# Cross-attention and a mixture of experts on one core: each group's attention starts four slots earlier in the order of work, the second group's in the head

## What is computed

```python
q = layernorm(x) @ Wq.T                      # [*, 128]
k = v = ctx @ Wq.T
x = x + softmax(causal(q @ k.T / sqrt(128))) @ v          # within each sequence of 64
n = layernorm(x)
gates = softmax(n @ gate_W)                  # 8 experts
cw = the two largest gates, divided by their sum, 0 elsewhere
out = n + sum_e cw[:, e] * (relu(n @ W1[e] + b1[e]) @ W2[e] + b2[e])   # hidden width 256
x = x + out
```

## Time and profile before

| | us |
|---|---|
| median of 3 runs | 143.75 (143.26 to 143.96) |
| profiled execution, its own time | 143.2 |
| span of that execution | 141.4 |
| PE busy | 125.1 (88%) |
| DVE busy | 104.9 (74%) |
| ACT busy | 96.2 (68%) |
| POOL busy | 47.3 (33%) |

### The profile page before, as it was taken

How to read it: one execution, slowest core, us unless ns; L and a number is a source line. 1 busy time by engine, 2 the same in 40 slices (tenths; PEclk the granted TensorE clock), 3 DMA queues, 4 the chain that set the end, 5 groups by cost and what they waited for, 6 DMA issues and landing times. The chain is left out here.

```text
span 141.4 us, 3259 instructions
## 1 busy us (share of the span) xinstructions
PE 125.1 (88%) x1165; PEld 92.9 (66%) x1165; DVE 104.9 (74%) x413; ACT 96.2 (68%) x191; POOL 47.3 (33%) x53
## 2 busy tenths in 40 slices
PE   6987079789999699999998799999996999699992
PEld 2774055658786457887875468697864677467781
DVE  1529999998559799476586995885497994978573
ACT  3346354976959486796959476769685848689940
POOL 6380342703033750330127532130336603333500
PEclk9999956999999999999999999999999999999999
DMA  3999900000000000200000001000000002000002
GB/s 107 293 270 270 270 4 5 0 0 2 0 5 0 0 7 0 74 0 5 0 0 0 0 5 53 28 0 0 0 5 2 2 5 74 0 2 5 0 0 74
DMA packets 9872, 5.54 MB, mean 39 GB/s; under 512 B 472, under 2 KB 9856, under 8 KB 9856
## 3 DMA queue, kind: packets, MB, share of 16 engines
q1 hardware_dynamic: 9712, 5.27, 12.9%
q10 hardware_dynamic: 144, 0.07, 0.2%
HBM read 4.28 MB, written 1.05 MB: 38 GB/s over the span
## 5 line engine op out<-in xcount | busy, mean ns | idle before, releaser
L623 POOL TENSOR_TENSOR h_lo<-h,h_hi 128x512 f16<-128x512 f32 x24 | 27.9, 1162 | 67.7 <-ACT h L517 67.7
L517 ACT ACTIVATE h<-psH,b1T 128x512 f32<-128x512 f32 x64 | 43.5, 686 | 3.1 <-PE psH L347 1.8
L790 DVE SCALAR_TENSOR_TENSOR acc<-psY,weight_y,acc 128x128 f32<-128x128 f32 x125 | 35.1, 342 | 5.8 <-PE psY L368 5.3
L516 ACT ACTIVATE h_hi<-psH,b1T 128x512 f16<-128x512 f32 x48 | 33.0, 687 | 9.1 <-PE psH L347 9.0
L774 DVE TENSOR_TENSOR h_lo<-h,h_hi 128x512 f16<-128x512 f32 x24 | 17.3, 721 | 15.2 <-ACT h L517 15.2
L347 PE MATMUL psH<-x_lo,w_hi 128*128 128x512 f16 x62 | 23.8, 384 | 0.4
L343 PE MATMUL psH<-x_hi,w_hi 128*128 128x512 f16 x62 | 23.8, 384 | 0.0
L344 PE MATMUL psH<-x_hi,w_lo 128*128 128x512 f16 x62 | 23.8, 383 | 0.0
L368 PE MATMUL psY<-w_hi,h_hi 128*128 128x128 f16 x192 | 22.7, 219 | 0.0
L368 PE MATMUL psY<-w_lo,h_hi 128*128 128x128 f16 x192 | 22.7, 219 | 0.0
L368 PEld LDWEIGHTS psY<-w_hi,h_hi 128*128 128x128 f16 x192 | 15.4, 98 | 3.3
(11 more groups left out here) (169 smaller groups left out, 184.3 us busy)
## 6 DMA issues: line engine op xcount, KB each, us to landing
w_sb<-in_L_ffn_W_dram SPq DMA_DIRECT2D x8, 256.0 KB, 5.1
x_sb<-in_x_dram SPq DMA_DIRECT2D x1, 768.0 KB, 6.9
ctx_sb<-in_ctx_dram SPq DMA_DIRECT2D x1, 768.0 KB, 6.5
out_dram<-acc SPq DMA_DIRECT2D x3, 256.0 KB, 2.3
x_sb<-in_x_dram SPq DMA_DIRECT2D x1, 256.0 KB, 3.5
ctx_sb<-in_ctx_dram SPq DMA_DIRECT2D x1, 256.0 KB, 3.9
out_dram<-acc SPq DMA_DIRECT2D x2, 128.0 KB, 1.8
wq_sb<-in_L_xattn_Wq_dram ACTq DMA_DIRECT2D x1, 64.0 KB, 2.6
```

Of the source, the lines that this page charges most:

```text
L516: nc.scalar.activation(h_hi[:, C * (e % 2) + c, :], psH[c][:, :], ACT.Relu, bias=bias, scale=scale)
L517: nc.scalar.activation(h[:, C * (e % 2) + c, :], psH[c][:, :], ACT.Relu, bias=bias, scale=scale).then_inc(h_ready, 1)
L623: nc.gpsimd.tensor_tensor(h_lo[:, i, :], h[:, i, :], h_hi[:, i, :], ALU.subtract).then_inc(hlo0_ready, 1)
L790: last = nc.vector.scalar_tensor_tensor(out=o, in0=y, scalar=weight_y[:, t, e:e + 1], in1=o, op0=ALU.mult, op1=ALU.add)
```

## The change

The steps of a group are now numbered over two groups: a step at slot s of group a stands behind slot s of group a - 2, where slots of 16 and more are those of group a - 1. `X_T` is 12 (it was 16 in this count), `KEYS` 13 (17), `VALUES` 14 (18), `SCORES` 15 (18), `PROBS_T` 18 (21), `ATTN` 20 (23), `NORM2` 23 (24), `XF_T` 26 (27), `LOGITS` 28 (30), and the choice and weights of the gate move from the start of the group into slots 30 and 31, ahead of it. For group 1 the steps up to the maximum are written into the head, on banks of their own (`FIRST_BANKS`), and its exponentials behind slot 0 of group 0. The steps of the weights need `weight_y` of two groups at once, so it gets two buffers. The statistics of groups 2 and 3 and the low parts of the weights of experts 4 to 7 move from the head into the loop, the last high parts on ScalarE from the head to slot 2, and the high parts of the second pair from ScalarE to GpSimd. The loads come as four tiles of x, four of the context, the first pair, four of x, four of the context, the small inputs, the other pairs, and the last eight tiles of each. The banks of keys, context and values change places, and the logits go to `psD`.

The full diff is longer; its core:

```diff
+        LOOP_BANKS = {"xT": psA, "ctxT": psC, "keysT": psB, "values": psC, "scores": psA, "probsT": psB, "attn": psA,
                       "xfT": psB}
         HEAD_BANKS = [{"ctxT": p, "xT": q, "keysT": r, "values": p, "scores": q, "probsT": r, "attn": s, "xfT": s}
                       for p, q, r, s in ((psH[0], psH[1], psC, psD), (psY[0], psY[1], psA, psB))]
+        FIRST_BANKS = dict(LOOP_BANKS, keysT=psY[1])
         LAST_BANKS = (psY[1], psA, psB, psC)
...
+        SLOTS = 2 * E
         CAT_T, B2_PRODUCT, B2_ADD = 3, 4, 5
-        X_T, KEYS, VALUES, SCORES, MAX, EXPS, PROBS_T, ATTN = 0, 1, 2, 2, 2, 3, 5, 7
-        RESIDUAL, NORM2, XF_T, X_LO, LOGITS, GATE_TOP = 7, 8, 11, 11, 14, 14
+        X_T, KEYS, VALUES, SCORES, PROBS_T, ATTN, XF_T, LOGITS = 12, 13, 14, 15, 18, 20, 26, 28
+        X_OUT, KEYS_OUT, VALUES_OUT, EXPS, PROBS_OUT, X_HI, GATE_EXP = 12, 13, 15, 16, 18, 26, 29
+        STATS, MAX, RESIDUAL, VARIANCE, NORM2, X_LO, GATE_TOP, CHOICE, WEIGHTS = 11, 15, 20, 21, 23, 26, 29, 30, 31
+        W1_LO = (3, 0, 2, 5)
+        W2_LO = (2, 0, 4, 8)
+        W_HI = (0, 0, 2, 2)
+        FIRST_RSTD, RSTD, BASE = 12, 21, 26
 
         def run(steps, slot):
-            for at, step in steps:
-                if at == slot:
-                    step()
+
+            for at, first, step in steps:
+                for a in range(first, GROUPS):
+                    if max(0, (a - 2) * SLOTS + at) == slot:
+                        step(a)
...
-            sp.dma_start(x_sb[:, TG:, :], x_v[:, TG:, :]).then_inc(x_in[1], 16)
+            sp.dma_start(x_sb[:, TG:2 * TG, :], x_v[:, TG:2 * TG, :]).then_inc(x_in[1], 16)
+            sp.dma_start(ctx_sb[:, TG:2 * TG, :], ctx_v[:, TG:2 * TG, :]).then_inc(ctx_in[1], 16)
             sp.dma_start(gate_sb[:, :], gate_w).then_inc(small_in, 16)
...
             weights(1)
-            sp.dma_start(ctx_sb[:, TG:, :], ctx_v[:, TG:, :]).then_inc(ctx_in[1], 16)
             for p in range(2, PAIRS):
                 weights(p)
+            sp.dma_start(x_sb[:, 2 * TG:, :], x_v[:, 2 * TG:, :]).then_inc(x_in[2], 16)
+            sp.dma_start(ctx_sb[:, 2 * TG:, :], ctx_v[:, 2 * TG:, :]).then_inc(ctx_in[2], 16)
 
             def store(g):
...
+            def key_step(a):
+                pe.wait_ge(xlo_ready, a * TG)
+                key_product(a, ALL, LOOP_BANKS)
+
+            def inputs_step(a):
+                pe.wait_ge(ctx_in[2], 16)
+                pe.wait_ge(x_in[2], 16)
+                ctx_transposes(a, ALL, LOOP_BANKS)
+                x_transposes(a, ALL, LOOP_BANKS)
...
+            steps = [(X_T, 2, inputs_step), (KEYS, 2, key_step), (VALUES, 2, lambda a: value_product(a, ALL, LOOP_BANKS)),
+                     (SCORES, 2, lambda a: score_product(a, ALL, LOOP_BANKS)), (PROBS_T, 1, probs_step),
+                     (ATTN, 1, lambda a: attention_product(a, ALL, LOOP_BANKS)),
+                     (XF_T, 1, lambda a: xf_transposes(a, ALL, LOOP_BANKS)), (LOGITS, 1, logit_product)]
+            group_steps = {CAT_T: cat_transposes, B2_PRODUCT: b2_product}
...
+            x_transposes(1, ALL, FIRST_BANKS)
             pe.wait_ge(ctx_in[1], 16)
-            pe.wait_ge(x_in[1], 16)
+            ctx_transposes(1, ALL, FIRST_BANKS)
+            key_product(1, ALL, FIRST_BANKS)
+            value_product(1, ALL, FIRST_BANKS)
             for ts, banks in HALVES:
                 xf_transposes(0, ts, banks)
+            score_product(1, ALL, FIRST_BANKS)
             pe.wait_ge(w1lo_ready, 1)
             for ts, banks in HALVES:
                 pe.wait_ge(xlo_ready, ts[-1] + 1)
...
-            w1_hi_part(1)
-            w2_hi_part(1)
+            x_out(1, ALL, FIRST_BANKS)
+            ctx_out(1, ALL, FIRST_BANKS)
+            keys_out(1, ALL, FIRST_BANKS)
+            values_out(1, ALL, FIRST_BANKS)
             for ts, banks in HALVES:
                 x_hi_part(0, ts, banks)
...
+            first_rstd(0)
+            weights_hi(0)
+            weights_hi(1)
             for ts, banks in HALVES:
                 attention_rstd(0, ts)
+            first_rstd(1)
             base_sum(0)
-            pool.wait_ge(var_ready, TILES)
-            first_rstd(TG, TILES - TG)
...
-                dve.wait_ge(y_used, Y_FREE + a * E)
-                nc.vector.tensor_scalar(weight_y[:, :, :], weight[:, :, :], 1.0 / (SH * SW), None, ALU.mult)
+                if a >= 2:
+                    dve.wait_ge(y_used, Y_FREE + (a - 1) * E)
+                if a >= 1:
+                    dve.wait_ge(catT_ps, a)
+                nc.vector.tensor_scalar(weight_y[:, a % 2, :, :], weight[:, :, :], 1.0 / (SH * SW), None, ALU.mult)
...
-                gate_choice(g, chain, [lambda: hidden_lo(g, 1), None, None, None])
-                gate_weights(g, chain)
+            def statistics(a):
+                dve.wait_ge(x_in[2], 16)
+                for t in range(a * TG, (a + 1) * TG):
+                    last = row_stats(t)
+                chain.link(last)
+                mean_and_var(a * TG, (a + 1) * TG, chain)
+
+            def residual_step(a):
+                invert_sums(a, ALL, chain)
+                residual_after(a, ALL, LOOP_BANKS)
+
+            def choice_step(a):
+                gate_choice(a, chain, None)
+
+            steps = [(STATS, 2, statistics), (MAX, 2, lambda a: mask_and_max(a, ALL, banks_of(a))),
+                     (RESIDUAL, 1, residual_step), (VARIANCE, 1, variance_step), (NORM2, 1, lambda a: second_norm(a, ALL)),
+                     (X_LO, 1, lambda a: x_lo_part(a, ALL, LOOP_BANKS)), (GATE_TOP, 1, lambda a: gate_top(a, chain)),
+                     (CHOICE, 1, choice_step), (WEIGHTS, 1, lambda a: gate_weights(a, chain))]
+
+            def after(g, slot):
+                run(steps, g * SLOTS + slot)
+                for p in range(2, PAIRS):
+                    if g == 0 and slot == W1_LO[p]:
+                        w1_lo_part(p)
+                    if g == 0 and slot == W2_LO[p]:
+                        w2_lo_part(p)
+                if slot == B2_ADD:
...
                 second_variance(0, ts, chain)
-            more_stats(TG, 2 * TG)
+            dve.wait_ge(x_in[1], 16)
+            for t in range(TG, 2 * TG):
+                last = row_stats(t)
+            chain.mark(last)
             for ts, banks in HALVES:
                 second_norm(0, ts)
+            chain.wait()
+            mean_and_var(TG, 2 * TG, chain)
             w2_lo_part(0)
             for ts, banks in HALVES:
                 x_lo_part(0, ts, banks)
-            chain.mark(more_stats(2 * TG, TILES))
+            mask_and_max(1, ALL, FIRST_BANKS)
             w1_lo_part(1)
-            w2_lo_part(1)
-            chain.wait()
-            mean_and_var(TG, TILES, chain)
-            hidden_lo(0, 0)
             gate_top(0, chain)
-            for p in range(2, PAIRS):
-                w1_lo_part(p)
-                w2_lo_part(p)
-            LINKS_BEFORE = chain.count
-            for g in range(0, GROUPS - 1):
-                inner = Chain(dve, dve_chain, LINKS_BEFORE + g * LINKS)
-                group(g, True, inner)
-                assert inner.count == LINKS, inner.count
-            group(GROUPS - 1, False, Chain(dve, dve_chain, LINKS_BEFORE + (GROUPS - 1) * LINKS))
+            gate_choice(0, chain, [lambda: w2_lo_part(1), lambda: hidden_lo(0, 0), None, None])
+            gate_weights(0, chain)
+            for g in range(GROUPS):
+                group(g)
```

More of the change, by code:

```diff
@@ L405, in group @@
                         hidden_product(g, e + 1)
-                    elif attention:
+                    elif g + 1 < GROUPS:
                         hidden_product(g + 1, 0)
-                    run(steps, 2 * e)
+                    after(g, 2 * e)
                     output_product(g, e)
-                    run(steps, 2 * e + 1)
+                    after(g, 2 * e + 1)
             pe.wait_ge(warm_zero, 1)
@@ L572, in _ @@
             gate_exps(0)
-            w1_hi_part(3)
-            w2_hi_part(3)
-            for g in range(0, GROUPS - 1):
-                group(g, True)
-            group(GROUPS - 1, False)
+            for g in range(GROUPS):
+                group(g)
         @block.gpsimd
@@ L818, in group, with after @@
+            def after(g, slot):
+                run(steps, g * SLOTS + slot)
+                for p in range(2, PAIRS):
[4 more added lines that the diff above has]
+                if slot == B2_ADD:
+                    add_b2(g)
+            def group(g):
                 for e in range(E):
-                    if 0 < e < E - 1:
+                    if e < E - 1:
@@ L820, in group @@
                         hidden_lo(g, e + 1)
-                    elif e and attention:
+                    elif g + 1 < GROUPS:
                         hidden_lo(g + 1, 0)
-                    run(steps, 2 * e)
+                    after(g, 2 * e)
                     add_expert(g, e)
-                    run(steps, 2 * e + 1)
+                    after(g, 2 * e + 1)
```

125 lines of the change are left out of this document (54 added, 71 removed).

## The result

The changed kernel takes 132.7 us (median of 4 runs, 132.47 to 133.15), the kernel before 143.5 on the same chip (142.99 to 143.96). The ratio is 0.925 [0.921, 0.930]. That is 0.6 us under the predicted 133.3; the profiled span is 130.8 us where 131.0 was forecast.

What follows compares the result with a forecast made beforehand. PE, busy 88% of the span, was taken to bound the kernel. Terms of 13.85 us removed and 3.4 added, net 10.4, took the span from 141.4 to 131.0 and the forecast median to 133.3 us, range 130.0 to 138.5.

Steps and rivals of the forecast that it cites:

- the context's transposes: Group 0: PE's wait for them to come out of PSUM goes with group 1's work; -1.6 us.
- xf: Loop, groups 0 to 2: PE's wait for xf goes because the norm comes in time; -5.7 us.
- x_lo: Loop, three groups: PE's wait for x_lo goes, as it comes two experts earlier than its reader; -0.9 us.
- the gate's weights: Group 3: PE's wait for them goes, as they are computed at the end of group 2; -1.4 us.
- rival 1: Loop: the waits for xf stay; 4.8 us more, 138.1 us; chance 0.17.
- the 0.4 charged for groups 1 and 2: Loop: 0.2 us of remaining xf wait charged in each of these groups, part of a +1.0 us term.
- The start of group 0: Head: the first full hidden product gains 0.7 us but pays for POOL holding DVE; +0.6 us in sum (-0.7 to +0.8).
- POOL's price: Head: DVE held up by POOL's high parts of the second pair; between 0 and 1.5 us, taken as 1.3.
- rival 3: Head: POOL does not hold DVE up; 1.3 us less, 132.0 us; chance 0.14.
- The charge for group 0: Group 0: new waits for exponentials 0.7, `weight_catT` 0.6 and xf 0.5; +1.8 us (0.5 to 4).
- The clock's term: Group 0: hidden product 1 runs at PE's full speed, 1.30 us instead of 1.95; -0.65 us.
- rival 2: Head or group 0: PE's clock falls all the same, PE loses 3.4 us; 136.7 us; chance 0.10.

Runs made afterwards that it cites:

- e10: Changed kernel with group 1's attention kept in the loop at its old slots, group 2's statistics at slot 12; 138.40 us, ratio 0.968 to the kernel before.
- a1: Changed kernel run again unchanged, as the measure for runs beside it; 132.34 us, ratio 0.924 to the kernel before.
- e7: Changed kernel with POOL's power for the second norm at slot 22 instead of 21, behind expert 4's h_lo; 131.80 us, ratio 0.920.
- e8: e7 with the gate's exponential at slot 30 instead of 29 and the last pair's high parts at slot 4 instead of 2; 131.50 us, ratio 0.916.
- e6: Changed kernel with the statistics of groups 2 and 3 back in the head, behind the maximum; 136.34 us, ratio 0.952 to the kernel before.
- e4: Changed kernel with the high parts of the second pair of weights on ACT again instead of POOL; 131.85 us, ratio 0.919.
- e12: Changed kernel with all moves of e8 and the edit of e4; 130.44 us, ratio 0.912 to the kernel before.
- e9: Changed kernel with only group 1's move to the head and the gate's early weights; later attention at old slots, statistics at 13; 140.52 us, ratio 0.982.
- e1: Kernel before with 13 products of zeros added in PE's idle time in the head; 142.58 us, ratio 0.997.
- e11: e10 with 13 products of zeros on PE in the head; its two executions near full clock took 135.94 and 136.26 us, ratio 0.951.

## Why the prediction was right

**The terms that are read off the trace came out to 0.1.** Group 1's work, the context's transposes, xf, x_lo and the gate's weights: each was a distance between two starts less the work's own pace, and each wait went whole. That the norm would be in time was the step with the largest price (rival 1, 4.8 us). It held, but by less than the 0.9 us claimed: DVE's xf of group 2 runs from 67.61 to 69.56, and PE's load of its last tile begins at 69.68 (69.35 is that of the first). The sum of 3.0 us for four additions and the norm was right (1.04 and 1.95, the norm held by POOL's h_lo as charged); the condition "if DVE isn't late" was not met. Expert 3's output product ended on PE at 65.75 (63.80 and 1.95), but b2's addition (65.24) and an h_lo (65.97) still stood in front of its addition, which began at 66.57. So 0.12 us were left, and the 0.4 charged for groups 1 and 2 did not fall due. e10 shows the same without the head's part: no wait for xf in groups 1 and 2. That the gate's weights are ready 1.7 us before PE reads them is seen in the trace; later ones were not tried.

**The reason given for xf named the wrong distance.** The prediction says that the norm "now" stands three slots in front of its reader, and that before 1.34 us less of PE's work lay between. But the slots are 24 and 27 before and 23 and 26 after: three in both. PE's work between them is the same, 77.16 - 73.13 = 4.0 us before (77.16 is 76.71 plus the 0.45 of its products) and 69.57 - 65.58 = 4.0 after. What grew is the distance in front of the norm, from the product with the values (slot 23, now 20) to it: on PE 73.13 - 70.95 = 2.2 us before, 65.58 - 60.04 = 5.5 after. Residual, variance and POOL's power have to run in it. Before, the norm waited 0.92 us for the power and began at 77.33, when PE was already due; after, the power is done at 66.45 (65.44 and 1.01) and DVE comes to the norm at 67.61 without idling. The price was right because it was read off PE's starts. No run moved the two distances apart.

**The context's wait may not need group 1's move.** The prediction has it go with group 1's work. In e10 this work is still in the loop and the wait is gone all the same; there PE comes later too, so it is not shown which of the two, PE's lateness or ACT's shorter queue, did it.

**The start of group 0 was mis-sized.** Predicted +0.6, measured -0.4. 0.4 of the difference is no effect of the change: the first transposes of probabilities, in front of everything that moved, began at 10.69 against 11.08, and from execution to execution this point lay between 9.73 and 11.16 in the profiles. Counted from it the first full hidden product stood at 11.44 us before and 11.43 after. The other 0.6 is POOL's price: I took 1.3 from the norm's row and it was 0.67 on DVE in after. In the length of the head it was 0.5 to 0.9: 11.43, 11.82, 11.69, 11.71 and 11.71 us in the profiles of after, a1, e7, e8 and e6, and 10.95 and 10.96 in e4 and e12, which have no `w_hi` of the second pair on POOL. The rest of the term was -0.5 (10.95 against 11.44), predicted -0.7. So the price lay between my forecast and rival 3, which said 0. The mechanism was right, `gate_hi` ending at 12.14, right behind POOL's `w_hi` (12.12). But it did not begin later: 1.09 us behind the first transposes of probabilities in both profiles (12.17 - 11.08 and 11.78 - 10.69).

The rule of the Trainium skill (page "SBUF — State Buffer", section "Who interferes with whom"), by which the low part, with its two SBUF inputs, is held as well, would have made it dearer. The traces bear it out in part: beside POOL's `w_hi`, `w_lo` took 0.68 in after, as it does alone (0.69), but 0.88 in e7, 0.87 in e9, 1.01 in a1 and 1.05 in e10, and never lasted until POOL was done (in a1 it ended at 11.22, `w_hi` at 11.55). What sets this apart no run shows. That page's other sentence, that whoever issues first gets the shared pair for the whole instruction, fits e9's h_lo, 1.60 for 0.69 where POOL was 0.10 us ahead. In e4, where it was 1.84 for 0.69, both began at once, and the trace can't tell who was first.

**The charge for group 0 was right in sum (1.8) and wrong in its parts.** The exponentials cost 0.5 and not 0.7, `weight_catT` 0.4 and not 0.6. The third, 0.5 for xf, did not come; in its place 0.9 for expert 4's h_lo on POOL, behind a power that waits for DVE. That the sum is 1.8 all the same is luck. And xf was hardly earlier than forecast: after PE had lost those 0.9 us, DVE's last xf ended at 41.16 and PE's load of it began at 41.20. I had the order of POOL's instructions and counted only DVE's and ACT's. The like on ACT cost 0.9 in group 3: the gate's exponential waits 2.53 us for `below`, with the activations of group 3's expert 0 behind it:

```profile
105.62 0.23 ACT L525 ACTIVATE gate_exp<-below 128x32 f32<-128x32 f32 x1 [2.53 <-DVE below L773]
```

Both are one rule, which the prediction applied neither to POOL nor to this exponential: an instruction that waits on a helper holds all that is queued behind it. e7 and e8 remove both.

**The clock's term was right for after, and its reason incomplete.** e1 shows that in the kernel before the clock was not on the path (0.15 us), e11 that in a kernel with the loop's moves alone it costs 2.3 us. (The 1.95 us that the prediction gives for a hidden product "at half speed" are one in which the clock rose again; e11's profile has 25.63 - 23.11 = 2.52 for one that was slow throughout.) The 0.65 was what one product shows; the change as a whole probably owes the clock more, since the loop's moves without the work in the head lose 2.3 us to it. No term of a sum made on the profile of before could show this, and it did not hurt because rival 2 did not come about.

**What stays open.** Of the 3.6 us by which both parts together exceed their sum, 2.3 are the clock. The rest is 1.3. The distances in the three profiles make it about 1.8: group 0's xf goes only where both parts are (1.9), the halves' own new waits come to 5.1 (e9) and 2.0 (e10) against 3.5 in after, and against that the waits for the gate's weights and the context (3.0) and the clock's 0.65 are counted in both halves. No run takes these apart. Which of these waits recur in the executions without a trace is open too.

## What to carry to other kernels

Make the ledger from start-to-start distances on the engine that leads, and not from bracketed waits; it also finds what has no bracket. Then list, for each helper engine that the change touches, what stands behind each waiting instruction: two of the three largest new waits here came from there, and moving one number each removed them. And do not price the parts of a change one by one if they share a leader: a slow stretch of the clock was worth next to nothing in the kernel before and 2.3 us where PE led behind it. Last, count a step's lead from where its inputs come, and not only from the step to its reader: here the first distance grew and the second did not.
